# A kernel of eight layers on one core: the output product moves to the bank of queries and keys, copies change places, and the two mixtures fill their gate chains with products

## The chip, the cores and the metric

The kernel runs on one core of a Trainium2 chip. The metric is the device time of one execution in microseconds (us). Before the change three timed runs took 1647.21, 1647.35 and 1652.68 us, median 1647.35. The profiled execution, from which all rows below are taken, took 1640.3 us; its span, from the first to the last instruction, is 1638.5 us, so 1.8 us lie around the span. Engines are named as in the profile: PE (TensorE matmul), PEld (TensorE weight load), DVE (VectorE), ACT (ScalarE), POOL (GpSimd).

## The reference

The input is 8 sequences of 256 tokens of 128 numbers, 2048 tokens in all, and a context of the same shape. Four attention layers and four feed-forward layers follow each other, each with a layer norm in front and a residual sum behind:

```
x = x + L0_xattn(layernorm(x), ctx, ctx)              # 16 heads of 8, causal
x = x + L0_ffn(layernorm(x), W1, b1, W2, b2)          # ternary weights, gelu
x = x + L1_xattn(layernorm(x), ctx, mask, ...)        # 16 heads of 64, row mask
x = x + L1_ffn(layernorm(x), ...)                     # product keys, top 8
x = x + L2_xattn(ctx, layernorm(x), ...)              # 16 heads of 8, biases, causal
x = x + L2_ffn(layernorm(x), w_red, wg, W1, b1, W2, b2)   # mixture, 1 of 8 experts, gelu
x = x + L3_xattn(layernorm(x), ctx, ctx, mask, ...)   # 16 heads of 64, key mask
x = x + L3_ffn(layernorm(x), gate_w, we_*, ws_*)      # mixture, 2 of 8 experts, 2 shared, silu
```

The two attention layers with 16 heads of 64 (L1 and L3) are the wide layers. In outline, for one head: `softmax(q @ k.T * 64**-0.5 + mask) @ v`, then all heads times the output weights. The mixture of L2 takes for each token the expert of the largest gate: `o = (gelu(x @ W1[e] + b1[e]) @ W2[e] + b2[e]) * score`. The mixture of L3 takes the two largest of 8 gates, each expert with a capacity of 640 tokens in order of arrival, and adds two shared experts that every token passes: `sh = silu(x @ ws_gate.T) * (x @ ws_up.T) @ ws_down.T`. Everything is float32.

## The kernel before, in words

All engines run a program written out by hand, in order, with semaphores between them: an instruction behind a wait stands still with its engine. The layers are stages one after the other: raw, ffn0, rows (the wide layer L1, 207 to 545 us), ffn1, bias, ffn2 (the mixture L2, 1011 to 1160), keys (the wide layer L3, 1161 to 1490), ffn3 (the mixture L3, 1493 to the end).

**A wide layer** goes over 8 batches (one sequence of 256 tokens each), 8 pairs of heads in a batch, two pairs in a step, so 4 steps u = 0 to 3 in a batch. Batch 0 and batch 7 are written out, batches 1 to 6 are a loop. A step of PE (`step` in `wide_tensor`) is: the scores of two pairs (L932, into banks 0 to 3), the product of weights and values of the step before last (`weighted`, L969, bank 6), one product of queries and keys (L898 and L899, bank 7), the transposes of a pair of the step before (L947: its four for i = 0 into bank 4, its four for i = 1 into bank 5), a product for the values (L911, bank 6), a second one of queries and keys, and a second pair's transposes. Step 2 then turns the normalised x of the next batch (`norm`, L888), and step 1 does the output product of the batch before (`out_product`, L919, 16 matmuls into bank 5). Because bank 5 is also the bank of the transposes for i = 1, the output product waits until ACT has copied these out (`w_pt[1]`, ACT L1046), and in the next step the transposes wait until DVE has added the product to x (`w_added`, DVE L1121).

DVE in a step: the maxima of both pairs (L1137, 8 instructions), the inverse of the first pair's sums (L1143), the copy of queries and keys (L1107), in step 0 the statistics of the next batch (L1257 to L218), the inverse of the second pair's sums, the copy of the first transposes (`copy_pt`, L1150, bank 4), the copy of the values (L1114), in step 2 the next batch's normalisation (`normalise`, L1096), the second `copy_pt`, in step 2 the copy of the turned x (`norm_out`, L1103) and the context, in step 1 the addition of the output product. ACT does the exponentials (L1036), the other half of the transposes (L1046), every second copy of queries and keys (L1027) and the heads' results (L1053). POOL multiplies by the inverses (L1213, two instructions of 128x512 for a pair) and does the Newton rounds for the norm's root (L1298 to L1304, four small instructions a round): two rounds in step 0, the third in step 1.

**A mixture** first normalises all 16 tiles, turns them (L1490), and makes the gate logits (L1898). Then DVE runs a chain of small instructions (the gate chain): the largest gates, their indices, a hand-over to ACT for the exponential (L1928), the sums and weights, and a split in three bf16 parts (L1992 to L1996). PE turns these (L1920) and ACT copies them to `gT` (L1931), which every group of 512 tokens needs to spread its gates (L2068, L2139). While DVE is in the chain, PE does four products ahead in ffn2 and two units' in ffn3, then waits. Four groups follow, group 0 written out, the others a loop. In ffn2 a group has 16 halves of experts: an up product (L1880), ACT's gelu, DVE's product with the gate, a down product (L2060). In ffn3 a group has 10 units, 8 experts and 2 shared ones: two up products (L1888 and L1889), ACT's silu (L2162), DVE's product with the up result (L2182) and with the gate (L2186), a down product (L2130); a shared unit has only one DVE product (L2189).

## Time and profile before

| | |
|---|---|
| timed runs, median of 3 | 1647.35 us (1647.21 to 1652.68) |
| profiled execution | 1640.3 us, span 1638.5 us, mean granted clock 0.958 |
| PE busy | 1413.3 us, 86% of the span |
| DVE, ACT, POOL busy | 1022.6, 898.7, 690.4 us |
| the chain that ended last | PE 61%, DVE 17%, ACT 12%, issue 8%, POOL 2% |
| one batch in the loop of the keys stage | 39.91 us |
| one group in the loop of ffn3 | 29.09 us |

Busy time is the time in which an engine had an instruction in work. A matmul of float32 is recorded as two PE records (x2 for one matmul), and matmuls overlap in the pipeline: eight records that last 1.04 us together are followed by the next instruction after less than that. In brackets stands the idle time of the engine ahead of an instruction and who ended it.

### The profile page before, as it was taken

Reading aid. Unit: us, or ns where it says so; the run is one execution under the profiler, and the core shown is the slowest. Engines: PE = TensorE matmul, PEld = TensorE weight load, DVE = VectorE, ACT = ScalarE, POOL = GpSimd, SP = SyncE. Lnnn points to the kernel's source line nnn. Section 1 sums busy time; section 2 is a strip of 40 time slices with the busy share of each in tenths; the row PEclk is TensorE's granted clock in tenths of the full one; section 3 lists DMA queues with packets and bytes.
Section 4 is the critical chain, followed back from the end, with each engine's and each line's share of the span. In section 5 each row is a group of like instructions: output and inputs, shape, how many; then the busy total and the mean of one; then the engine's idle time right before and its main releaser. Section 6 shows DMA issues by size and latency. Waiting matters only on the chain.

```text
span 1638.5 us, 30033 instructions
## 1 busy us (share of the span) xinstructions
PE 1413.3 (86%) x9437; PEld 937.4 (57%) x9449; DVE 1022.6 (62%) x3380; ACT 898.7 (55%) x1867; POOL 690.4 (42%) x1056
## 2 busy tenths in 40 slices
PE   5996889999998577868778895899899999996998
PEld 2443457777766476767654443444576777664343
DVE  5653366666665799998955554433566666655444
ACT  3665456666665477777746663333566666661222
POOL 5341144444443589989853331000344444441000
PEclk9999899999999689998999997999999999997999
DMA  2016000000000000000000000000000000000000
GB/s 66 17 49 252 4 4 5 3 3 3 3 3 1 26 1 1 1 0 0 1 1 1 1 2 1 26 1 0 4 4 4 3 3 6 0 1 1 7 6 13
DMA packets 12665, 21.76 MB, mean 13 GB/s; under 512 B 3088, under 2 KB 9120, under 8 KB 11936
## 3 DMA queue, kind: packets, MB, share of 16 engines
q1 hardware_dynamic: 12576, 20.63, 3.5%
q8 instruction: 49, 0.80, 0.2%
q14 instruction: 40, 0.33, 0.1%
HBM read 19.58 MB, written 1.05 MB: 13 GB/s over the span
## 4 chain that ended last, share of the span: by engine, by line
PE 61%; DVE 17%; ACT 12%; issue 8%; POOL 2%; DVEq 0%; ACTq 0%; DMA 0%; SPq 0%; POOLq 0%
PE bank L932 7%; PE bank L969 6%; PE bank L947 5%; DVE sb_both L1841 4%; PE bank L919 4%; ACT sb_both L1036 4%; PE bank L1880 3%; PE bank L2060 3%; PE bank L898 3%; PE bank L409 2%; PE bank L1888 2%; PE bank L451 2%; PE bank L1889 2%; PE bank L899 2%; PE bank L2130 2%
## 5 line engine op out<-in xcount | busy, mean ns | idle before, releaser
L1213 POOL TENSOR_TENSOR sb_both<-sb_both,sb_winv 128x512 f32<-128x512 f32 x256 | 260.8, 1040 | 323.7 <-DVE sb_winv L1143 323.7
L1036 ACT ACTIVATE sb_both<-sb_both,sb_wneg 128x256 f32<-128x256 f32 x512 | 253.0, 495 | 151.0 <-DVE sb_wneg L1137 150.9
L1768 POOL TENSOR_TENSOR sb_KM<-sb_OT 128x1024 f32<-128x1024 f32 x128 | 240.2, 1913 | 31.8 <-DVE sb_both L1841 27.8
L1672 PE MATMUL bank<-sb_ident,sb_both 128*128 128x128 f32 x1024 | 139.4, 286 | 59.3 <-DVE sb_both L1841 37.0
L1137 DVE CUSTOM_DVE_ANT_0 sb_both<-bank,sb_pen 128x256 f32<-128x256 f32 x512 | 182.1, 420 | 0.0
L1298 POOL TENSOR_TENSOR sb_ntmp<-sb_rstd 128x2 f32<-128x2 f32 (+2 forms) x123 | 24.2, 197 | 340.6 <-DVE sb_rstd L218 335.3
L1841 DVE SCALAR_TENSOR_TENSOR sb_both<-sb_KM,sb_best,bank 128x1024 f32<-128x1024 f32 x128 | 158.4, 1273 | 11.3 <-ACT bank L1743 11.3
L1672 PEld LDWEIGHTS bank<-sb_ident,sb_both 128*128 128x128 f32 x1024 | 119.2, 147 | 73.6 <-DVE sb_both L1841 47.4
L1743 ACT ACTIVATE bank<-sb_KM 128x1024 f32<-128x1024 f32 x128 | 129.6, 1023 | 35.3 <-DVE sb_both L1841 30.2
L947 PE MATMUL bank<-sb_ident,sb_both 128*128 128x128 f32 x1024 | 134.4, 274 | 12.2 <-DVE sb_QT L1150 12.1
L947 PEld LDWEIGHTS bank<-sb_ident,sb_both 128*128 128x128 f32 x1024 | 116.3, 141 | 36.0 <-issue 20.0
L969 PE MATMUL bank<-sb_QT,sb_VP 128*64 128x256 f32 x1024 | 127.7, 392 | 3.2 <-DVE sb_QT L1150 3.2
L932 PE MATMUL bank<-sb_KM 64*128 64x256 f32 x1024 | 128.1, 390 | 0.0
L932 PEld LDWEIGHTS bank<-sb_KM 64*128 64x128 f32 x1024 | 93.8, 187 | 19.6 <-issue 8.6
L1150 DVE COPY sb_QT<-bank 128x512 f32<-128x512 f32 x128 | 88.1, 688 | 24.3 <-PE bank L947 24.0
L969 PEld LDWEIGHTS bank<-sb_QT,sb_VP 128*64 128x64 f32 x1024 | 69.8, 139 | 52.1 <-issue 20.8
L1036 ACT ACTIVATION_READ_ACCUMULATOR sb_both<-sb_both,sb_wneg 128x1 f32 x512 | 95.9, 187 | 0.0
L1046 ACT ACTIVATE sb_QT<-bank 128x512 f32<-128x512 f32 x128 | 75.1, 587 | 35.3 <-PE bank L947 35.3
L2116 DVE TENSOR_TENSOR sb_both<-bank,sb_both 128x512 f32<-128x512 f32 x64 | 44.0, 691 | 74.1 <-ACT sb_both L2095 48.7
L692 DVE TENSOR_REDUCE sb_VP<-bank 128x4 f32<-128x1024 f32 (+1 forms) x48 | 58.7, 1223 | 36.2 <-PE bank L415 36.0
L583 ACT ACTIVATE sb_xnT_all<-bank 128x1024 f32<-128x1024 f32 x48 | 49.0, 1022 | 52.2 <-PE bank L415 52.2
L2095 ACT ACTIVATE sb_both<-bank,sb_f1b 128x512 f32<-128x512 f32 x64 | 43.6, 687 | 61.5 <-PE bank L1880 61.5
(273 smaller groups left out, 2731.0 us busy)
## 6 DMA issues: line engine op xcount, KB each, us to landing
sb_ctxT_in<-in_ctxT SPq DMA_DIRECT2D x24, 128.0 KB, 2.3
sb_F<-in_F SPq DMA_DIRECT2D x2, 1024.0 KB
sb_XO<-in_ctx SPq DMA_DIRECT2D x8, 128.0 KB, 2.0
sb_WKQ<-in_WKQ SPq DMA_DIRECT2D x1, 1024.0 KB, 9.0
sb_W1ALL<-in_ctxT SPq DMA_DIRECT2D x1, 1024.0 KB, 4.7
sb_xn_all<-in_keymask SPq DMA_DIRECT2D x1, 1024.0 KB, 4.3
out_x<-sb_x SPq DMA_DIRECT2D x4, 256.0 KB, 2.3
sb_x<-in_x SPq DMA_DIRECT2D x1, 896.0 KB, 4.7
```

The source lines that it names most:

```text
L932: last = pe.matmul(s[:, h, i, :], QK[rows, t, 0, i * P:(i + 1) * P], QK[rows, t, 1, :], start=True, stop=True)
L947: last = pe.transpose(bank[4 + i][:, n * P:(n + 1) * P], PRW[:, t % 4, h, i, kt * P:(kt + 1) * P], ident[:])
L969: last = pe.matmul(bank[6][rows, (t % 2) * SEQ:(t % 2 + 1) * SEQ], VW[:, kt, (2 * t + h) * 64:(2 * t + h + 1) * 64], PTW[:, t % 2, h, kt, ...
L1036: last = act.activation(p, p, ACT.Exp, scale=-1.0, bias=wneg[:, t % 4, h, i:i + 1], accum_out=wsum[:, t % 4, h, i:i + 1])
L1046: act.activation(PTW[:, t % 2, :, :, P:2 * P], bank[5][:].rearrange("p (h i q) -> p h i q", h=2, i=TPB), ACT.Copy).then_inc(w_pt[1], 1)
L1137: dve.tensor_tensor_reduce(PRW[:, t % 4, h, i, :], s[:, h, i, :], mask, -1.0, BIG, ALU.add, ALU.min, wneg[:, t % 4, h, i:i + 1]).then_inc( ...
L1150: dve.tensor_copy(PTW[:, t % 2, :, :, 0:P], bank[4][:].rearrange("p (h i q) -> p h i q", h=2, i=TPB))\
L1213: pool.tensor_tensor(p, p, winv[:, t % 4, :, i:i + 1].broadcast_to([P, 2, SEQ]), ALU.mult).then_inc(w_norm, 1)
L1672: last = pe.matmul(weight_bank(c), gated[:, h % 4, c * P:(c + 1) * P], ident[:], is_transpose=True, start=(h == 0 and c % 4 == 0), stop=(h ...
L1743: act.activation(sig_bank(h), pairsum[:, h % 4, :], ACT.Sigmoid).then_inc(sig_ready, 1)
L1768: pool.tensor_tensor(dst, s[:, h, 0, :].unsqueeze(2).broadcast_to([P, NK, NK]), s[:, h, 1, :].unsqueeze(1).broadcast_to([P, NK, NK]), ALU. ...
L1841: dve.scalar_tensor_tensor(out=gated[:, h % 4, :], in0=pairsum[:, h % 4, :], scalar=best[:, t % 2, h, TOPK - 1:TOPK], in1=sig_bank(h), op0 ...
```

## The change

In the wide layers the output product goes to bank 7, the bank of queries and keys, and waits for the copy of the sixth pair's queries and keys in place of ACT's copy of the transposes; the next product that uses bank 7 after it, that of pair 6 in step 2, waits for the addition. On DVE the first `copy_pt` stands ahead of the second inverse, and `normalise` moves from the middle of step 2 to step 1, ahead of the addition. POOL does all three Newton rounds in step 0.

In ffn2, PE does all 16 up products of group 0 while the gate chain runs, ACT puts their gelu into 16 buffers of their own (`first_acts`, in KM and VP), and takes the gate's exponential after the fifth gelu and the copies of `gT` after the eleventh. In ffn3 the two shared experts leave the groups and are done for all tokens ahead of them, among the steps of the gate chain: PE's up products, ACT's silu and a copy of the up result, POOL's product, PE's down product (with the tokens on the rows, so nothing has to be turned back), ACT's copy, and POOL's addition to x. A group has then 8 units.

```diff
@@ wide_tensor
+                if j == 6 and not known_below(b, 1):
+                    pe.wait_ge(w_added, A.batches + b)
                 pe.matmul(bank[7][:, 0:SEQ], WQ[:, j * P:(j + 1) * P], xnT[:], start=True, stop=True)
...
-            def out_product(b, turned):
+            def out_product(b, copied):
                 pe.wait_ge(w_ot, heads(b + 1, 0))
-                pe.wait_ge(w_pt[1], A.pairs + turned)
+                pe.wait_ge(w_qk_out, A.pairs + copied)
...
-                        last = pe.matmul(bank[5][:, i * D:(i + 1) * D], OT[:, j, i * P:(i + 1) * P], WO[:, j, :],
+                        last = pe.matmul(bank[7][:, i * D:(i + 1) * D], OT[:, j, i * P:(i + 1) * P], WO[:, j, :],
...
-                    if t == 2 and i == 1 and not known_below(b, 1):
-                        pe.wait_ge(w_added, A.batches + b)
...
-                    out_product(b - 1, PAIRS * b + 2)
+                    out_product(b - 1, PAIRS * b + 6)
@@ wide_vector, step
+                if behind or u >= 1:
+                    bt, ut = steps_back(b, u, 1)
+                    copy_pt(bt, 2 * ut)
                 inverses(b, 2 * u + 1)
                 if u == 3 and more:
                     penalty(b + 1)
-                if behind or u >= 1:
-                    bt, ut = steps_back(b, u, 1)
-                    copy_pt(bt, 2 * ut)
                 if u < 3:
                     values(b, u + 1)
                 elif more:
                     values(b + 1, 0)
-                if u == 2 and more:
-                    normalise(b + 1)
                 if behind or u >= 1:
                     copy_pt(bt, 2 * ut + 1)
+                if u == 1 and more:
+                    normalise(b + 1)
@@ wide_pool, step
                 if u == 0 and part != "last":
-                    rsqrt(pool, 0, TPB, A.ln + b + 1, [0, 1])
-                if u == 1 and part != "last":
-                    rsqrt(pool, 0, TPB, A.ln + b + 1, [2])
+                    rsqrt(pool, 0, TPB, A.ln + b + 1)
@@ ffn2 and ffn3
+    EXP_AFTER2, GATE_AFTER2 = 4, 10
+    def shared_down(pe, g):
+        pe.wait_ge(sh_prod, 2 * g + 2)
+        if g >= 2:
+            pe.wait_ge(sh_out, g - 1)
+        for i in range(TPG):
+            for u in range(2):
+                last = pe.matmul(bank[4 + g % 2][:, i * P:(i + 1) * P],
+                                 gated_ring[:, (2 * g + u) % 4, i * P:(i + 1) * P], SD[:, u, :],
+                                 start=(u == 0), stop=(u == 1))
+        last.then_inc(sh_down, 1)
+    def shared_act(act, q):
+        u = q % 2
+        act.wait_ge(sh_up, q + 1)
+        if q >= 4:
+            act.wait_ge(sh_prod, q - 3)
+        act.activation(act_ring[:, q % 4, :], bank[2 * u][:], ACT.Silu)
+        act.activation(shared_u[:, q % 4, :], bank[2 * u + 1][:], ACT.Copy).then_inc(sh_act, 1)
...
+        for q in range(2 * GROUPS):
+            product(q)                      # POOL: shared_u * act_ring -> gated_ring
+            if q >= 5 and q % 2 == 1:
+                add((q - 5) // 2)           # POOL: x += shared_out
...
@@ tensor2
-        gate_tensor(pe, A)
+        gate_logits(pe, A)
+        for n in range(16):
+            up2(pe, 0, n)
+            if n == GATE_AFTER2:
+                gate_turn(pe, A, 4)
+        pe.wait_ge(gT_ready, 2)
@@ scalar2, body
+                if known_zero(g) and n == EXP_AFTER2:
+                    gate_exp(act, A)
+                if known_zero(g) and n == GATE_AFTER2:
+                    gate_out(act, A, 4)
@@ scalar3
-        gate_scalar(act, A)
+        shared_act(act, 0)
+        shared_act(act, 1)
+        gate_exp(act, A)
+        shared_act(act, 2)
...
+        shared_evac(act, 1)
+        gate_out(act, A, 6)
+        shared_act(act, 6)
...
```

The first place is DVE in step 2 and step 1 of a batch of the keys stage (`sb_QT` is where the transposed weights go, `sb_VP` the values, `sb_xn` the normalised x of the next batch, `sb_xnT` its transpose). Step 2 before:

```order
L1107 COPY sb_KM<-bank 128x512
L1143 RECIPROCAL sb_winv<-sb_wsum 128x4
L1149 REGISTER_ALU
L1150 COPY sb_QT<-bank 128x4x128
L1111 REGISTER_ALU
L1114 COPY sb_VP<-bank 128x512
L1094 ISA
L1096 TENSOR_SCALAR sb_xn<-sb_x,sb_mv,sb_rstd 128x128 x2
L1149 ISA
L1150 COPY sb_QT<-bank 128x4x128
L1100 REGISTER_ALU
```

Step 1 of the changed kernel, on DVE, from the same copy of queries and keys to the addition:

```order
L1107 COPY sb_KM<-bank 128x512
L1149 REGISTER_ALU
L1150 COPY sb_QT<-bank 128x4x128
L1143 RECIPROCAL sb_winv<-sb_wsum 128x4
L1111 REGISTER_ALU
L1113 REGISTER_ALU
L1114 COPY sb_VP<-bank 128x512
L1149 ISA
L1150 COPY sb_QT<-bank 128x4x128
L1094 ISA
L1096 TENSOR_SCALAR sb_xn<-sb_x,sb_mv,sb_rstd 128x128 x2
L1117 REGISTER_ALU
```

The first copy to `sb_QT` moved ahead of the inverse, and the two instructions that write `sb_xn` stood between the values and the second copy in step 2; they now stand behind the second copy of step 1, with the wait of the addition (L1117) next.

The second place is ACT in ffn2 between the four copies of the turned x and group 0's end. In the changed kernel (`sb_g_e` is the exponential of the gates; ACT_TABLE_LOAD changes the function table; the kernel before has one in this stage, ahead of the first gelu and behind the copies of `gT`):

```order
L1499 ACTIVATE sb_xnT_all<-bank 128x512 x4
L2155 ACT_TABLE_LOAD
L2155 ACTIVATE sb_KM<-bank,sb_f1b 128x512 x5
L1978 ACT_TABLE_LOAD
L1978 ACTIVATE sb_g_e<-sb_g_t 128x128
L2155 ACT_TABLE_LOAD
L2155 ACTIVATE sb_KM<-bank,sb_f1b 128x512 x3
L2155 ACTIVATE sb_VP<-bank,sb_f1b 128x512 x3
L1984 ACTIVATE sb_gT<-bank 128x1024 x2
L2155 ACTIVATE sb_VP<-bank,sb_f1b 128x512 x5
L2163 ACTIVATE sb_outT<-bank 128x512
```

The gate's exponential moved behind five gelus, and it has a table change on each side. In ffn3 it stands in the same way behind two silus and two copies.

## Rows read from the trace of the kernel before

**Rows 1.** Windows: span, then PE, PEld, DVE, ACT, POOL busy, clock, DMA.
```profile
1256.77:1296.68 39.91, 38.04 (x266) 28.02 (x267) 26.63 (x111) 24.79 (x80) 18.57 (x28) 1.00 0.01 3
...
1507.00:1511.00 4.00, 4.00 (x18) 1.99 (x16) 3.51 (x15) 0.00 (x0) 0.00 (x0) 0.50 0.00 0
...
1518.00:1524.60 6.60, 5.87 (x8) 2.47 (x9) 1.97 (x3) 0.00 (x0) 0.00 (x0) 0.50 0.00 0
...
1545.27:1574.36 29.09, 28.34 (x70) 12.49 (x72) 13.05 (x19) 6.57 (x11) 0.00 (x0) 1.00 0.02 9
```
**Rows 2.** Timeline of PE, keys stage: start, duration, instruction, [idle before <-releaser].
```profile
1269.61 0.43 PE L888 MATMUL bank<-sb_ident,sb_xn 128*128 128x128 f32 x2 [0.69 <-DVE sb_xn L1096]
...
1274.74 1.04 PE L947 MATMUL bank<-sb_ident,sb_both 128*128 128x128 f32 x8
1275.62 1.02 PE L911 MATMUL bank<-sb_WV,sb_ctxT 128*128 128x512 f32 x2
...
1286.39 1.06 PE L947 MATMUL bank<-sb_ident,sb_both 128*128 128x128 f32 x8 [0.40 <-DVE sb_QT L1150]
...
1296.68 3.81 PE L919 MATMUL bank<-sb_WO,sb_OT 128*128 128x128 f32 x32 [0.78 <-ACT sb_QT L1046]
```
**Rows 3.** Timeline of DVE in the same batch.
```profile
1268.14 1.33 DVE L1096 TENSOR_SCALAR sb_xn<-sb_x,sb_mv,sb_rstd 128x128 f32 x2
...
1285.39 0.17 DVE L1143 RECIPROCAL sb_winv<-sb_wsum 128x4 f32<-128x4 f32 x1
1285.56 0.69 DVE L1150 COPY sb_QT<-bank 128x512 f32<-128x512 f32 x1
...
1300.66 0.43 DVE L1121 TENSOR_TENSOR sb_x<-bank,sb_x 128x256 f32 x1 [4.46 <-PE bank L919]
```
**Rows 4.** Timeline of POOL in the same batch.
```profile
1285.64 2.04 POOL L1213 TENSOR_TENSOR sb_both<-sb_both,sb_winv 128x512 f32<-128x512 f32 x2 [0.68 <-DVE sb_winv L1143]
1287.64 0.19 POOL L1298 TENSOR_TENSOR sb_ntmp<-sb_rstd 128x2 f32<-128x2 f32 x1
...
1289.55 0.19 POOL L1304 TENSOR_TENSOR sb_rstd<-sb_rstd,sb_ntmp 128x2 f32<-128x2 f32 x1
```
**Rows 5.** Timeline of ACT in the same batch.
```profile
1294.97 0.60 ACT L1027 ACTIVATE sb_KM<-bank 128x512 f32<-128x512 f32 x1 [0.62 <-PE bank L899]
```
**Rows 6.** Timeline of PE at the gate chain and group 0's start of ffn2.
```profile
1028.73 5.85 PE L1880 MATMUL bank<-sb_xnT_all,sb_F 128*128 128x512 f32 x8
1035.89 1.07 PE L1920 MATMUL bank<-sb_identB,sb_QT 128*128 128x128 bf16 x16 [1.31 <-DVE sb_QT L1996]
1038.77 0.38 PE L2068 MATMUL bank<-sb_gT,sb_sel 128*128 128x512 bf16 x1 [1.81 <-ACT sb_gT L1931]
...
1041.26 1.13 PE L2060 MATMUL bank<-sb_both,sb_F 128*128 128x512 f32 x2 [1.47 <-DVE sb_both L2116]
```
**Rows 7.** Timeline of ACT, the table change ahead of the first gelu of ffn2.
```profile
1038.50 1.28 ACT L2095 ACT_TABLE_LOAD   x1
1039.80 2.42 ACT L2095 ACTIVATE sb_both<-bank,sb_f1b 128x512 f32<-128x512 f32 x4
```
**Rows 8.** Timeline of DVE, the first instruction behind the exponential in ffn2.
```profile
1033.49 0.29 DVE L1969 TENSOR_REDUCE sb_gs_z<-sb_g_e 128x16 f32<-128x128 f32 x1
```
**Rows 9.** Timeline of PE in ffn3: gate chain, first down product, last of group 0.
```profile
1506.53 0.29 PE L1906 MATMUL bank<-sb_picks,sb_before 128*128 128x128 bf16 x1 [5.29 <-DVE sb_picks L1967]
...
1515.60 0.38 PE L2139 MATMUL bank<-sb_gT,sb_sel 128*128 128x512 bf16 x1 [1.81 <-ACT sb_gT L1931]
1518.73 2.07 PE L2130 MATMUL bank<-sb_both,sb_WD 128*128 128x512 f32 x2 [2.75 <-DVE sb_both L2186]
...
1545.27 1.13 PE L2130 MATMUL bank<-sb_both,sb_SD 128*128 128x512 f32 x2 [0.61 <-DVEq L2192]
...
1560.07 0.38 PE L2139 MATMUL bank<-sb_gT,sb_sel 128*128 x1
...
1562.86 0.38 PE L2139 MATMUL bank<-sb_gT,sb_sel 128*128 x1
```

More of the change, by code:

```diff
@@ L1883, in up3 @@
     def up3(pe, g, n):
-        if not (known_zero(g) and n < 2):
-            pe.wait_ge(prod_step, UNITS * g + n - 1)
-        wgate, wup, _ = unit_weights(n)
-        pe.matmul(bank[2 * (n % 2)][:], wgate, xnT_all[:, bass.ts(g, GROUP)], start=True, stop=True)
-        pe.matmul(bank[2 * (n % 2) + 1][:], wup, xnT_all[:, bass.ts(g, GROUP)],
-                  start=True, stop=True).then_inc(up_done[3], 1)
-    def gate_tensor(pe, A):
+        if known_zero(g) and n < 2:
+            pe.wait_ge(sh_act, 2 * GROUPS - 1 + n)
+        else:
+            pe.wait_ge(prod_step, EXPERTS * g + n - 1)
@@ new lines, in up3, with shared_up @@
+        pe.matmul(bank[2 * (n % 2)][:], WG[:, n, :], xnT_all[:, bass.ts(g, GROUP)], start=True, stop=True)
+        pe.matmul(bank[2 * (n % 2) + 1][:], WU[:, n, :], xnT_all[:, bass.ts(g, GROUP)],
+                  start=True, stop=True).then_inc(up_done[3], 1)
+    def shared_up(pe, q):
+        g, u = q // 2, q % 2
+        if q >= 2:
+            pe.wait_ge(sh_act, q - 1)
+        pe.matmul(bank[2 * u][:], SG[:, u, :], xnT_all[:, g * GROUP:(g + 1) * GROUP], start=True, stop=True)
+        pe.matmul(bank[2 * u + 1][:], SU[:, u, :], xnT_all[:, g * GROUP:(g + 1) * GROUP],
+                  start=True, stop=True).then_inc(sh_up, 1)
@@ new lines, in shared_evac, with pool3, product, add @@
+    def shared_evac(act, g):
+        act.wait_ge(sh_down, g + 1)
+        act.activation(shared_out[:, g, :], bank[4 + g % 2][:], ACT.Copy).then_inc(sh_out, 1)
+    def pool3(pool, A):
+        def product(q):
+            pool.wait_ge(sh_act, q + 1)
+            if q >= 4:
+                pool.wait_ge(sh_down, (q - 4) // 2 + 1)
+            pool.tensor_tensor(gated_ring[:, q % 4, :], shared_u[:, q % 4, :], act_ring[:, q % 4, :], ALU.mult)\
+                .then_inc(sh_prod, 1)
+        def add(g):
+            pool.wait_ge(sh_out, g + 1)
+            xg = x[:, TPG * g:TPG * g + TPG, :]
+            pool.tensor_tensor(xg, xg, shared_out[:, g, :].rearrange("p (i d) -> p i d", i=TPG), ALU.add)\
+                .then_inc(sh_added, 1)
+        for q in range(2 * GROUPS):
+            product(q)
+            if q >= 5 and q % 2 == 1:
+                add((q - 5) // 2)
+        add(GROUPS - 2)
+        add(GROUPS - 1)
@@ L1900, in gate_tensor, with gate_counts, gate_turn @@
         last.then_inc(lg_done, 1)
-        if k == 1:
-            pe.wait_ge(count_done, 1)
-            flat = picks[:].rearrange("p t e -> p (t e)")
-            width = TILES * EXPERTS
-            pe.matmul(bank[7][:, 0:width], before[:], flat, start=True, stop=True)
-            for n in range(1, TILES):
-                last = pe.matmul(bank[7][:, n * EXPERTS:width], onesB[:], flat[:, 0:width - n * EXPERTS],
-                                 start=False, stop=True, skip_group_check=True)
-            last.then_inc(count_done, 1)
-        if k == 0:
-            for n in range(UPS_AHEAD2):
-                up2(pe, 0, n)
-        else:
-            for n in range(UNITS_AHEAD3):
-                up3(pe, 0, n)
-        pe.wait_ge(parts_ready, k + 1)
+    def gate_counts(pe):
+        pe.wait_ge(count_done, 1)
+        flat = picks[:].rearrange("p t e -> p (t e)")
+        width = TILES * EXPERTS
+        pe.matmul(bank[7][:, 0:width], before[:], flat, start=True, stop=True)
+        for n in range(1, TILES):
+            last = pe.matmul(bank[7][:, n * EXPERTS:width], onesB[:], flat[:, 0:width - n * EXPERTS],
+                             start=False, stop=True, skip_group_check=True)
+        last.then_inc(count_done, 1)
+    def gate_turn(pe, A, first):
+        pe.wait_ge(parts_ready, A.index - 1)
         for i in range(TILES):
-            home = bank[4 + i // 8][:].bitcast(BF16)
+            home = bank[first + i // 8][:].bitcast(BF16)
             last = pe.transpose(home[:, (i % 8) * P:(i % 8 + 1) * P], parts[:, i, :], identB[:])
@@ L2125, in tensor3 @@
         norm_tensor(pe, A)
[L2126 removed]
+        gate_logits(pe, A)
+        for q in range(4):
+            shared_up(pe, q)
+        gate_counts(pe)
+        shared_down(pe, 0)
+        shared_up(pe, 4)
+        shared_up(pe, 5)
+        shared_down(pe, 1)
+        gate_turn(pe, A, 6)
+        shared_up(pe, 6)
+        shared_up(pe, 7)
+        shared_down(pe, 2)
+        shared_down(pe, 3)
+        pe.wait_ge(gT_ready, 4)
+        pe.wait_ge(sh_out, GROUPS - 1)
         def down(g, n):
[L2129 to L2130 removed]
+            pe.wait_ge(gated_done[1], EXPERTS * g + n + 1)
+            pe.matmul(bank[6][:], WD[:, n, :], gated_ring[:, n % 4, :], start=(n == 0), stop=(n == EXPERTS - 1))\
               .then_inc(down_done[1], 1)
         def body(g):
[L2134 to L2142 removed]
+            for n in range(EXPERTS):
+                if known_zero(g) and n == 1:
+                    pe.wait_ge(sh_out, GROUPS)
+                if not (known_zero(g) and n < 2):
+                    pe.wait_ge(gated_done[1], EXPERTS * g + n - 1)
+                pe.matmul(bank[4 + n % 2][:], sel[:, n, :], gT[:, bass.ts(g, GROUP)],
+                          start=True, stop=True).then_inc(bc_done[1], 1)
+                up3(pe, g, n)
                 if n == 1 and not known_zero(g):
@@ L2146, in body @@
                     down(g, n - 1)
-            down(g, UNITS - 1)
+            down(g, EXPERTS - 1)
         groups(pe, body)
@@ L2226, in pool @@
             pool1(pool_, A)
+        if A.kind == "ffn3":
+            pool3(pool_, A)
     F.early_stats = early_stats
```

101 lines of the change are left out of this document (50 added, 51 removed).

## The prediction

> **What bounds the kernel now.** I read the windows first, then the timeline of PE with its idle times, then the other engines around each idle time. In the loop of a wide layer a batch takes 39.91 us, and PE has an instruction in work for 38.04 of them at the full clock [rows 1]; DVE, ACT and POOL are at 26.6, 24.8 and 18.6 us. So PE is the bound, and the 1.87 us left are three idle times that the timeline names: 0.69 us ahead of the turning of the next batch's x, 0.40 us ahead of a second transpose, 0.78 us ahead of the output product [rows 2]. They add up to 1.87 exactly, so nothing else of size is lost there. In the mixtures PE stands still around the gate chain: 1.31, 1.81 and 1.47 us in ffn2 [rows 6], and 5.29, 1.81 and 2.75 us in ffn3 [rows 9]. In ffn3 each group also ends in 0.61 us of waiting.
>
> **Wide layers, the output product.** It waits for ACT's copy of bank 5 [rows 2], which can only start when the transposes are through. In bank 7 it waits for the sixth copy of queries and keys, which ACT begins at 1294.97 and ends at 1295.57 [rows 5]. PE would be free at about 1295.65: the idle time goes but for a few hundredths. With it goes the tail of the pipeline: eight transposes last 1.04 us, but 0.88 us later the next instruction starts [rows 2], so a stop behind them costs 0.16 us more than the idle time shown. 0.78 + 0.16 = 0.94 us. The next user of bank 7 is the first product of step 2, behind scores and weighting, 3.9 us later; the addition takes 0.43 us right behind the product [rows 3]. That new wait is covered by over 3 us.
>
> **The norm.** The two instructions of 1.33 us stand ahead of the second copy in step 2, and PE waits for them, 0.69 us [rows 2, 3]. In step 1 they come in front of the addition, where DVE is idle for 4.46 us [rows 3]; they cost nothing there. They need the Newton rounds to be through. The second pair's multiplication on POOL starts up to 0.6 us later, since its inverse now stands behind a copy (0.69 us): 1285.64 becomes about 1286.25, it ends at 1288.3, and three rounds at 1.1 us (two last from 1287.64 to 1289.74) end at 1291.6 [rows 4]. The norm asks at about 1296: 4 us to spare. POOL's next pair waits in any case for the first inverse of step 1, some eight maxima into that step, and its product is turned only a step later. Gain 0.69 + 0.16 = 0.85 us.
>
> **The copy ahead of the inverse.** In step 0 the copy starts 0.17 us earlier, at the inverse's place, 1285.39 [rows 3], and PE's idle 0.40 us shrinks by that. In steps 1 to 3 the inverse waits for ACT's exponentials in any case, so the copy fits in front of it. Small gaps ahead of the second transposes there, and the slower refilling of the pipeline behind each stop, bear no name in the trace; I put 0.3 us on them, an estimate from the other stops' tails of 0.16 us.
>
> Sum for a batch: 0.94 + 0.85 + 0.17 + 0.3 = 2.3 us (2.26), lower bound 1.6 (idle times alone), upper 2.5. The loop has six batches; batch 0 has the norm but no output product and batch 7 the reverse, so I count 7.2 batches in each of two wide layers: 14.4 x 2.3 = 33 us (23 to 36).
>
> **ffn2.** Nothing is added on PE, only moved. Twelve up products of 0.86 us (half a pair of up and down products, of which the sixteen pieces below 1041.26 are full) go from group 0 into the gaps. What ACT does now sets the pace. The fifth gelu ends at about 1036.1; a change of tables takes 1.28 us [rows 7] and the exponential 0.3, so it ends at 1037.7 where it was through at 1033.4 before. From there DVE needs 1035.89 - 1033.49 = 2.4 us to the parts [rows 6, 8]: 1040.2. The next table change ends at 1039.0, and the tenth up product, which needs the sixth gelu's bank, starts at 1039.75 instead of 1038.7: one idle time of 1.05 us. PE turns the parts at 1041.5, when they have long been ready. ACT copies gT behind the eleventh gelu until 1044.6, which PE needs at 1046.7. The first down product comes at about 1047.9. Before it came at 1041.26, with twelve up products of 0.86 us = 10.3 us still to do, that is 1051.6 in this count. Gain 3.7 us (0.8 to 4.6).
>
> The price of a change of tables decides this term. The row shows 1.28 us, with the gelu 1.30 us behind the start of the load [rows 7]. The Trainium skill, "ScalarE: Activation LUTs", section "What ACT_TABLE_LOAD costs", gives about 1.28 us for the load plus some 1.38 us to drain, 2.66 us for every switch; by that the two added changes of ffn2 would delay the tenth up product by 2.8 us and the gain would be 0.9 us, and in ffn3 about 2 us would go. The trace shows no such drain ahead of or behind the load, so I go by the row.
>
> **ffn3.** A unit takes 1562.86 - 1560.07 = 2.79 us on PE, of which 0.22 is the spreading of the gate; a shared unit has 2.57 [rows 9]. Two leave each group: 5.14 us of 29.09 [rows 1]. But the group now ends with an expert, whose last down product waits for two products of DVE in a row in place of one: 0.61 becomes about 1.4 us, +0.8. A group gets 4.35 us shorter, four groups 17.4 us. Ahead of them come 16 up products, 13.8 us, and 32 small down products at 3.75 / 16 = 0.234 us as the output product has them [rows 2], 7.5 us: together 21.3 us. They fill 5.29 + 1.81 + 2.75 = 9.85 us of idle time. Because PE stood still, the first down product of group 0 took 2.07 us where 1.13 is the rule [rows 9]: the granted clock was 0.50, its lower level of 1.2 GHz, from 1507 to 1511 and from 1518 to 1524.6 us, with 4.00 + 5.87 us of PE in work [rows 1], of which half is the price: 5 us. In the changed kernel only the first two shared pairs run so, about 2.5 us. Rests remain: 0.7 us ahead of the last shared down product (its last product is POOL's, 1.02 us [rows 4], behind ACT), 0.4 us at the first expert, 0.3 elsewhere. The exponential is 3 us late and the parts come at 1514.5, PE asks at 1517.8. Sum: -17.4 - 9.85 - 5 + 21.3 + 2.5 + 1.4 = -7 us (-11 to 0).
>
> POOL's eight products lie beside DVE's chain. The Trainium skill, "SBUF — State Buffer", section "SBUF: two separate sides", says that POOL and a VectorE instruction with two SBUF inputs lock each other out of a shared pair of ports for whole instructions. No row here shows it; if it held, the chain could wait for up to three products, 3 us, which the 3.3 us to spare just cover.
>
> **Sum.** 33 + 3.7 + 7 = 43.7 us off the profiled execution's 1640.3 us, that is 1596.6 us. The timed runs' median lies 7 us above the profiled execution, so the forecast for the median is 1647.35 - 43.7 = 1603.6, rounded to 1603 us, 2.7% faster.
>
> **Rivals.**
> *A wait takes the place of the ones removed* (the copy of queries and keys by ACT for the output product, or DVE's addition, or the heads' copy ahead of the values): half the wide gain, 16 us, goes, and the time is 1619. For it: ACT's copy ends within 0.1 us of the point where PE asks. Against: all other slacks that I find are 0.2 us and more in a step of 8.4 us.
> *The mixtures give nothing*, because of the clock, the tables or the longer end of a group: 1647.35 - 33 = 1614. For it: the term of ffn3 is a difference of large numbers.
> *The moves in the wide layers don't do what they say*, PE's idle times only get other names: 1647.35 - 11 = 1636.
> *Slower.* The norm in step 1 waits for POOL's three rounds, and behind it on DVE stand the addition and the maxima of step 2; PE's product of pair 6 waits for the addition. If POOL's twelve small instructions came 4 us late, DVE would hold the loop, and from 7.5 us late on each of 14 batches would lose 3.1 us more than the mixtures and the rest give: 1650 to 1680, say 1660. Against: 4 us to spare before the first 0.1 us is lost, and POOL is busy for 18.6 of 39.9 us [rows 1].
>
> **How the numbers follow.** Forecast 0.72, half the wide gain 0.11, mixtures give nothing 0.09, moves without effect 0.04, slower 0.04. The range of 8 in 10 takes the bounds of the wide term (23 to 36) and of the mixtures (1 to 15), and some us by which executions of one kernel differ here: 1590 to 1619. A measurement of this kernel can tell about 0.5%, 8 us, from no change. Only the slower rival and a part of the fourth case lie at or above 1639: faster 0.93, same 0.03, slower 0.04.
>
> **What would show it.** A batch of the loop should last 37.6 us, with only 0.2 to 0.3 us of idle time left on PE, ahead of a second transpose in step 0; the output product with no idle time ahead of it, or one named by the copy of queries and keys. DVE's norm should come about 0.1 us behind a copy, with POOL's last round well before. In ffn2 one idle time of about 1 us within the up products and the first down product 18 to 20 us behind the first up product. In ffn3 three groups of 24.7 us with 1.4 us of waiting at the end, and the first expert's down product about 37 us behind the first turning of x. I am wrong if the loop's period stays above 38.5 us, or if a table change costs clearly over 1.3 us.

## The result and the profile after

The changed kernel takes 1603.43 us, median of four runs (1600.34 to 1607.1), beside 1647.28 us for the kernel before, also of four (1646.96 to 1652.68): the ratio is 0.9723, with a 95% interval of 0.970 to 0.9746. That is 43.85 us less. The profiled execution took 1600.34 us with a span of 1598.5 us, 40.0 us less than the one of before.

The windows of the changed kernel, columns as in [rows 1]: a batch in the loop of the keys stage, the gate logits of ffn2, the first shared up products of ffn3, and a group in the loop of ffn3.

```profile
1236.51:1274.32 37.81, 37.41 (x268) 28.20 (x267) 26.22 (x112) 24.78 (x80) 18.60 (x29) 1.00 0.01 3
1010.43:1017.11 6.68, 6.68 (x33) 6.68 (x33) 0.11 (x1) 1.88 (x2) 0.00 (x0) 0.50 0.42 158
1468.09:1473.90 5.81, 5.81 (x8) 2.50 (x9) 5.38 (x54) 1.08 (x2) 0.78 (x1) 0.51 0.00 1
1519.02:1543.54 24.52, 23.13 (x59) 10.24 (x61) 11.66 (x17) 5.37 (x9) 0.00 (x0) 1.00 0.03 11
```

A batch lost 2.10 us [rows 1], a group 4.57. The timeline of PE in a batch of the loop, at the places of [rows 2]:

```profile
1265.08 1.06 PE L947 MATMUL bank<-sb_ident,sb_both 128*128 128x128 f32 x8 [0.40 <-DVE sb_QT L1150]
...
1285.44 1.04 PE L947 MATMUL bank<-sb_ident,sb_both 128*128 128x128 f32 x8
1286.31 0.38 PE L888 MATMUL bank<-sb_ident,sb_xn 128*128 128x128 f32 x2
...
1311.27 1.04 PE L947 MATMUL bank<-sb_ident,sb_both 128*128 128x128 f32 x8
1312.14 3.82 PE L921 MATMUL bank<-sb_WO,sb_OT 128*128 128x128 f32 x32
```

The turning of the next x (L888) and the output product (L921) follow their transposes by 0.87 us with no idle time; the 0.40 us of step 0 stands as it stood. Summed from the starts of such rows in both traces, the 2.10 us are 0.97 for the output product, 0.92 for the norm, 0.13 and 0.08 for two gaps without a name ahead of second transposes.

By stage, from the first turning of x to the next stage's first (us; rows and keys are the wide layers):

| | rows | ffn1, bias | ffn2 | keys | ffn3 | before rows |
|---|---|---|---|---|---|---|
| before | 335.0 | 477.9 | 141.5 | 332.2 | 144.9 | 206.9 |
| changed | 318.4 | 477.9 | 139.7 | 315.1 | 138.0 | 209.5 |
| saved | 16.6 | 0.0 | 1.8 | 17.2 | 7.0 | -2.6 |

The last column is a warning for all that follows: no edit touches the work ahead of rows, yet in the thirteen profiled executions of this study it ended anywhere from 206.9 to 215.1 us. So whole times of single executions differ by up to 8 us without any edit; lengths of stages and periods of loops are what tells kernels apart. The loop periods repeat to 0.02 us.

### The profile page after: what moved, and what is told of

It reads as the page before. It is cut to its first block, busy times and chain, and to the rows that moved or that the text cites. A ratio compares the mean times of both kernels' runs of the same rounds, so it can differ in the third digit from the quotient of the medians.

```text
span 1598.5 us, 30106 instructions
## 1 busy us (share of the span) xinstructions
PE 1406.6 (88%) x9483; PEld 945.5 (59%) x9497; DVE 1023.4 (64%) x3372; ACT 909.5 (57%) x1883; POOL 706.3 (44%) x1068
## 3 DMA queue, kind: packets, MB, share of 16 engines
HBM read 19.58 MB, written 1.05 MB: 13 GB/s over the span
## 4 chain that ended last, share of the span: by engine, by line
PE 68%; DVE 15%; ACT 9%; issue 6%; POOL 1%; DVEq 0%; DMA 0%; ACTq 0%; SPq 0%; POOLq 0%
PE bank L934 7%; PE bank L969 7%; PE bank L947 6%; DVE sb_both L1846 4%; PE bank L900 4%; PE bank L921 4%; PE bank L1879 3%; PE bank L2118 3%; PE bank L901 3%; PE bank L913 3%; PE bank L409 2%; PE bank L451 2%; ACT sb_KM L598 2%; ACT sb_both L598 2%; ACT bank L1748 2%
## 5 line engine op out<-in xcount | busy, mean ns | idle before, releaser
L969 PE MATMUL bank<-sb_QT,sb_VP 128*64 128x256 f32 x1024 | 124.6, 385 | 3.2 <-DVE sb_QT L1150 1.6
L969 PEld LDWEIGHTS bank<-sb_QT,sb_VP 128*64 128x64 f32 x1024 | 68.6, 136 | 50.9 <-issue 21.9
L1027 ACT ACTIVATE sb_KM<-bank 128x512 f32<-128x512 f32 x64 | 38.2, 597 | 58.2 <-PE bank L901 58.1
L1107 DVE COPY sb_KM<-bank 128x512 f32<-128x512 f32 x64 | 44.1, 690 | 39.8 <-PE bank L901 39.8
```

The lines of the kernel that those rows point to most:

```text
L969: last = pe.matmul(bank[6][rows, (t % 2) * SEQ:(t % 2 + 1) * SEQ], VW[:, kt, (2 * t + h) * 64:(2 * t + h + 1) * 64], PTW[:, t % 2, h, kt, ...
```

## The experiments

Two parts of the change alone, each timed several times beside the kernel before, which took 1649.31 us there.

**wide_only.** The file before with every edit of the wide layers and none of the mixtures.

> The kernel before with the wide layers' part alone. My theory: the edits of the wide layers and of the mixtures don't touch each other, so rows and keys are as short as in the changed kernel (318.4 and 315.1 us instead of 335.0 and 332.2), ffn2 and ffn3 stay at 141.5 and 144.9 us; 34 us off, 1613. Rival, that a part of the mixtures' gain comes from the other state in which the clock reaches them: ffn2 or ffn3 moves by 2 us or more without any edit of its own.

Measured: 1615.42 us, ratio 0.979 (0.9756 to 0.9823), 33.9 us off. rows 318.3, keys 316.4 us, and a batch of keys 37.82. But ffn2, in which nothing is changed, took 143.97 us where it had taken 141.53. The rival's condition holds. The timeline of its PE shows where:

```profile
1014.87 1.12 PE L1488 MATMUL bank<-sb_ident,sb_xn_all 128*128 128x128 f32 x4 [0.66 <-DVE sb_xn_all L1481]
1015.78 6.83 PE L1896 MATMUL bank<-sb_gateW,sb_xnT_all 128*128 128x8 f32 x32
1022.46 6.73 PE L1878 MATMUL bank<-sb_xnT_all,sb_F 128*128 128x512 f32 x8
```

and the same place in the trace of the kernel before:

```profile
1023.57 0.66 PE L1490 MATMUL bank<-sb_ident,sb_xn_all 128*128 128x128 f32 x4 [0.66 <-DVE sb_xn_all L1483]
1024.07 4.81 PE L1898 MATMUL bank<-sb_gateW,sb_xnT_all 128*128 128x8 f32 x32
```

The gate logits took 6.83 us at a granted clock of 0.50 (1.2 GHz) and 4.81 us at 0.75, that is partly at 2.4 GHz, behind the same 8.51 and 0.66 us of idle time. In twelve of thirteen profiled executions they took 6.8 us; the one of before was the exception. What lies ahead of them is the same, so it is the moment at which the clock comes back that differs.

**mix_only.** The file before with the edits of ffn2 and ffn3 alone.

> The kernel before with the mixtures' part alone. My theory: ffn2 and ffn3 take 139.7 and 138.0 us as in the changed kernel, all else stays; 9 us off, 1638. Of ffn2, 2 us hang on whether its gate logits run at the lower clock for 4.8 or 6.8 us, which no edit decides: 137.7 if they take 4.8 us here. Rival: the mixtures give nothing by themselves, 1647.

Measured: 1637.96 us, ratio 0.9933 (0.9907 to 0.9959), 11.35 us off. The stages: ffn2 140.0 us with the logits at 6.8, ffn3 136.5 us (1.5 us less than expected, see the clock below); a batch of keys 39.92. The two parts add up to within 1.4 us: 33.9 + 11.35 = 45.2 beside 43.85.

The next six undo, move or leave out one thing in the changed kernel, one execution each; they are read by the lengths of stages and loop periods.

**bank5.**
```diff
-                pe.wait_ge(w_qk_out, A.pairs + copied)
+                pe.wait_ge(w_pt[1], A.pairs + copied)
...
-                        last = pe.matmul(bank[7][:, i * D:(i + 1) * D], OT[:, j, i * P:(i + 1) * P], WO[:, j, :],
+                        last = pe.matmul(bank[5][:, i * D:(i + 1) * D], OT[:, j, i * P:(i + 1) * P], WO[:, j, :],
...
+                    if t == 2 and i == 1 and not known_below(b, 1):
+                        pe.wait_ge(w_added, A.batches + b)
...
```


> The changed kernel with the output product back in bank 5, with its old waits, on all engines. My theory: PE waits again 0.78 us for ACT's copy of the transposes, and with the pipeline's tail a batch of the loop takes 0.97 us more, 38.8 instead of 37.81. Rival, that the other edits of the wide layers already give the copy its time: the idle time is under 0.4 us and the batch under 38.3 us.

Measured: a batch of 38.76 us, +0.94, with this row of its PE:

```profile
1287.94 3.81 PE L919 MATMUL bank<-sb_WO,sb_OT 128*128 128x128 f32 x32 [0.78 <-ACT sb_QT L1046]
```

The idle time of [rows 2] is back to the hundredth: the bank was its cause, and the other edits don't lend it time.

**norm2.**
```diff
+                if u == 2 and more:
+                    normalise(b + 1)
                 if behind or u >= 1:
                     copy_pt(bt, 2 * ut + 1)
-                if u == 1 and more:
-                    normalise(b + 1)
```


> The changed kernel with the normalisation back in step 2, ahead of the second copy; POOL still does all three rounds in step 0. My theory: its two instructions lie again beside POOL's products of 1.02 us and take 1.33 us instead of 0.59, since the two engines shut each other out; PE waits 0.7 us for them, and a batch takes 0.92 us more, 38.7. Rival, that the third round on POOL in step 1 was what slowed them: they take 0.59 us, PE waits under 0.1 us, and a batch takes 37.9.

Measured: a batch of 38.48 us, +0.66; the rows of its DVE, PE and POOL:

```profile
1295.11 1.40 DVE L1096 TENSOR_SCALAR sb_xn<-sb_x,sb_mv,sb_rstd 128x128 f32 x2
```
```profile
1296.64 0.43 PE L888 MATMUL bank<-sb_ident,sb_xn 128*128 128x128 f32 x2 [0.44 <-DVE sb_xn L1096]
```
```profile
1294.39 2.04 POOL L1213 TENSOR_TENSOR sb_both<-sb_both,sb_winv 128x512 f32<-128x512 f32 x2 [0.22 <-DVE sb_winv L1143]
```

The two instructions take 1.40 us beside POOL's products and end 0.08 us behind them, with all Newton rounds in step 0: the rival is out. The idle time is 0.44 and not 0.7 us, since DVE comes to the norm 0.3 us earlier, counted from PE's transposes: before, the first of the two instructions was held until POOL's second product ended (1.08 us) and the second followed it (0.33 us); here the first slips in (0.40 us) and only the second is held (1.08 us). All the durations of that line in the keys stage, in the trace before and in the one after (ns, min/median/max), show the same:

```profile
L1096 DVE TENSOR_SCALAR sb_xn<-sb_x,sb_mv,sb_rstd x14: 333/704/1091, 1188.4 to 1428.8; 128x128 f32 x12, 128x128 f32<-128x128 f32 x2
```
```profile
L1096 DVE TENSOR_SCALAR sb_xn<-sb_x,sb_mv,sb_rstd x12: 338/341/346, 1199.1 to 1388.4; 128x128 f32 x12
```

**copy_behind.**
```diff
-                if behind or u >= 1:
-                    bt, ut = steps_back(b, u, 1)
-                    copy_pt(bt, 2 * ut)
                 inverses(b, 2 * u + 1)
...
+                if behind or u >= 1:
+                    bt, ut = steps_back(b, u, 1)
+                    copy_pt(bt, 2 * ut)
```


> The changed kernel with the first copy of transposes behind the second inverse again, as before. The prediction's account: 0.17 us of step 0 and most of 0.3 us of unnamed gaps come back, a batch of 38.2 to 38.3 us. What the changed kernel's trace says: the idle time of 0.40 us in step 0 did not move, so only the gaps of 0.13 and 0.08 us ahead of second transposes can come back, 38.0 at most. Rival: the order of these two makes no difference at all, 37.81.

Measured: a batch of 37.99 us in keys (+0.18) and 37.97 in rows (+0.08), with the same 0.40 us in step 0. So in the loop the order gives the small gaps and nothing in step 0. Its DVE there, and below it that of the changed kernel:

```profile
1315.56 0.17 DVE L218 TENSOR_SCALAR sb_rstd<-sb_vbits 128x2 int32<-128x2 uint32 x1
1315.64 0.17 DVE L1143 RECIPROCAL sb_winv<-sb_wsum 128x4 f32<-128x4 f32 x1
1315.80 0.69 DVE L1150 COPY sb_QT<-bank 128x512 f32<-128x512 f32 x1
```
```profile
1264.00 0.17 DVE L218 TENSOR_SCALAR sb_rstd<-sb_vbits 128x2 int32<-128x2 uint32 x1
1264.24 0.69 DVE L1150 COPY sb_QT<-bank 128x512 f32<-128x512 f32 x1
```

The copy starts 0.24 us behind L218 with or without the inverse between them. The inverse lay in a gap that is there anyway.

Outside the loop the order is worth more. The keys stage took 321.0 us beside 315.1, the rows stage 322.5 beside 318.4, and most of that lies in the last batch, where PE has no products for a next step to do meanwhile: from the seventh output product to the eighth it is 31.88 us in keys and 32.30 in rows, beside 28.40 and 28.39. PE and DVE of copy_behind there, in keys:

```profile
1458.66 1.59 PE L947 MATMUL bank<-sb_ident,sb_both 128*128 128x128 f32 x8 [2.35 <-DVE sb_QT L1150]
1461.05 3.68 PE L969 MATMUL bank<-sb_QT,sb_VP 128*64 128x256 f32 x16 [0.79 <-DVE sb_QT L1150]
```
```profile
1457.75 0.18 DVE L1143 RECIPROCAL sb_winv<-sb_wsum 128x4 f32<-128x4 f32 x1 [2.08 <-ACT sb_both L1036]
```

and PE and DVE of the changed kernel:

```profile
1442.56 0.63 PE L947 MATMUL bank<-sb_ident,sb_both 128*128 128x128 f32 x4 [0.51 <-POOL sb_both L1213]
1444.07 0.63 PE L947 MATMUL bank<-sb_ident,sb_both 128*128 128x128 f32 x4 [0.89 <-ACT sb_QT L1046]
1445.49 1.95 PE L969 MATMUL bank<-sb_QT,sb_VP 128*64 128x256 f32 x16 [0.79 <-issue]
```
```profile
1441.72 0.69 DVE L1150 COPY sb_QT<-bank 128x512 f32<-128x512 f32 x1 [0.32 <-PE bank L947]
```

In the old order the copy stands behind an inverse that waits 2.08 us for ACT's exponentials, and PE stands still for 2.35 us; in the new order the stop is 0.51 and 0.89 us. The product behind it (L969) ran at a granted clock of 0.50 in copy_behind and at 1.00 in the changed kernel, 3.68 us instead of 1.95. Over all thirteen profiled executions, both wide stages, it took 3.3 to 3.7 us in six of six stages with the old order (before, mix_only, copy_behind) and in two of twenty with the new one (rows of norm2, 3.48; keys of stats_late, 3.60). So the longer stop and the lower clock behind it go with the order of these two instructions.

**stats_late.**
```diff
-                if u == 0 and more:
-                    norm_stats(dve, A, b + 1)
                 if behind or u >= 1:
                     bt, ut = steps_back(b, u, 1)
                     copy_pt(bt, 2 * ut)
                 inverses(b, 2 * u + 1)
+                if u == 0 and more:
+                    norm_stats(dve, A, b + 1)
```


> The changed kernel with the statistics of the next batch, in step 0, behind the first copy and the second inverse instead of ahead of them. My theory: the copy of bank 4 waits for DVE's 1.5 us of statistics, so the idle time of 0.40 us ahead of the second transposes goes, with 0.16 us of tail: a batch of 37.25 us, and some 8 us off the whole. Rival, that the delay only moves: the copy of the values and the second copy come 1.5 us later, the maxima of step 1 start late, and a batch takes 37.8 us or more.

Measured: a batch of 37.63 us, 0.19 less instead of 0.56. The 0.40 us is gone, and a new wait stands in step 1. DVE, then PE:

```profile
1316.33 0.36 DVE L212 TENSOR_SCALAR sb_veps<-sb_mv 128x2 f32<-128x2 f32 x1
1316.61 0.16 DVE L213 TENSOR_SCALAR sb_vhalf<-sb_mv 128x2 f32<-128x2 f32 x1
1316.80 0.90 DVE L215 TENSOR_SCALAR sb_vbits<-sb_veps 128x2 uint32<-128x2 uint32 x1
...
1318.54 0.68 DVE L1150 COPY sb_QT<-bank 128x512 f32<-128x512 f32 x1
```
```profile
1319.55 1.95 PE L969 MATMUL bank<-sb_QT,sb_VP 128*64 128x256 f32 x16 [0.30 <-DVE sb_QT L1150]
```

Instructions of 0.17 us took 0.36 and 0.90 us beside POOL's products (1315.63 to 1317.67), so the second copy came late. The wait moved, as the rival had it, but the trace puts 0.9 us of DVE's delay down to POOL; stats_early, below, tests that. Not all small instructions were held: the norm's statistics (L1255) took 0.29 and 0.28 us and their merging (L1259) 0.18 and 0.15 us beside the first of these products, as they do without one.

**parts_first.**
```diff
         for q in range(2 * GROUPS):
+            if q == 2:
+                pool.wait_ge(parts_ready, A.index - 1)
             product(q)
@@ tensor3 (scalar3 in the same order)
-        shared_down(pe, 1)
         gate_turn(pe, A, 6)
         shared_up(pe, 6)
         shared_up(pe, 7)
+        shared_down(pe, 1)
```


> The changed kernel, ffn3: POOL's products from the third on wait for the parts of the gates, and PE turns the parts ahead of the second shared down product. My theory, that POOL's products hold up DVE's chain by shutting it out of SBUF: from the first instruction behind the exponential to the end of the parts 5.2 us, as in the kernel before, instead of 9.2; no DVE instruction of the chain over 0.3 us; PE's 0.97 us ahead of the turning goes, and ffn3 is 1 to 2 us shorter. Rival, that the long instructions have another cause (weight loads, ACT's reads): the chain still takes 8 us or more.

In the changed kernel the chain behind the exponential looks like this on DVE:

```profile
1477.39 0.28 DVE L2022 TENSOR_REDUCE sb_gs_z<-sb_g_e 128x16 f32<-128x128 f32 x1 [2.87 <-ACT sb_g_e L1978]
...
1479.88 1.37 DVE L2035 TENSOR_TENSOR sb_g_oh<-sb_g_oh,sb_gs_w 128x128 f32<-128x128 f32 x1
1481.29 1.24 DVE L2036 TENSOR_TENSOR sb_g_comb<-sb_g_oh 128x128 f32<-128x128 f32 x1
...
1483.48 1.34 DVE L2046 TENSOR_TENSOR sb_g_r<-sb_g_comb,sb_QT 128x128 f32<-128x128 f32 x1
...
1485.44 1.17 DVE L2049 CAST sb_QT<-sb_g_r 128x128 bf16<-128x128 f32 x1
```

and POOL at the same time:

```profile
1479.84 2.55 POOL L1930 TENSOR_TENSOR sb_both<-sb_VP,sb_both 128x512 f32<-128x512 f32 x2 [2.75 <-ACT sb_VP L1919]
1483.40 1.27 POOL L1930 TENSOR_TENSOR sb_both<-sb_VP,sb_both 128x512 f32<-128x512 f32 x1 [1.02 <-ACT sb_VP L1919]
1485.12 1.41 POOL L1930 TENSOR_TENSOR sb_both<-sb_VP,sb_both 128x512 f32<-128x512 f32 x1 [0.45 <-ACT sb_VP L1919]
```

Each long instruction of DVE starts 0.05 to 0.32 us after a product of POOL has started and ends 0.08 to 0.15 us behind it; their neighbours take 0.29 us or less. With the products held back, DVE of parts_first:

```profile
1475.44 0.28 DVE L2024 TENSOR_REDUCE sb_gs_z<-sb_g_e 128x16 f32<-128x128 f32 x1 [1.49 <-ACT sb_g_e L1980]
...
1477.93 0.29 DVE L2037 TENSOR_TENSOR sb_g_oh<-sb_g_oh,sb_gs_w 128x128 f32<-128x128 f32 x1
...
1480.41 0.23 DVE L2051 CAST sb_QT<-sb_g_r 128x128 bf16<-128x128 f32 x1
```

The chain takes 1480.64 - 1475.44 = 5.20 us instead of 1486.61 - 1477.39 = 9.22. The expectation holds for the chain, and the rival is out. PE turns the parts without waiting. From the first turning of x to the first expert's down product it is 36.86 us; bank5 and group_end, whose ffn3 front is the changed kernel's and whose clock came back at the same point, take 37.82: 0.96 us gained, the 0.97 us of idle time, at the lower end of the 1 to 2 us expected.

**no_switch.**
```diff
-        act.activation(gt["e8"][:], gt["t1"][:], ACT.Exp).then_inc(gexp_done, 1)
+        act.activation(gt["e8"][:], gt["t1"][:], ACT.Gelu if A.index == 2 else ACT.Exp).then_inc(gexp_done, 1)
```


> The changed kernel, with the exponential of ffn2's gate replaced by a gelu, so the gates have other values; it leaves out two table changes of ACT in ffn2. By the row of 1.28 us for a change: ACT's sixth gelu comes 2.6 us earlier, PE's idle time of 0.96 us ahead of the tenth up product goes, and ffn2's group 0 ends 1.1 us earlier. If a change cost 2.66 us (load and drain), the sixth gelu would come 5.3 us earlier, and more than 2 us of idle time of PE would have to be found in the changed kernel that goes here.

ACT of the changed kernel around the exponential of ffn2:

```profile
1023.05 0.69 ACT L2155 ACTIVATE sb_KM<-bank,sb_f1b 128x512 f32<-128x512 f32 x1 [0.17 <-PE bank L1879]
1023.75 1.28 ACT L1978 ACT_TABLE_LOAD   x1
1025.05 0.31 ACT L1978 ACTIVATE sb_g_e<-sb_g_t 128x128 f32<-128x128 f32 x1
1025.37 1.28 ACT L2155 ACT_TABLE_LOAD   x1
1026.67 1.84 ACT L2155 ACTIVATE sb_KM<-bank,sb_f1b 128x512 f32<-128x512 f32 x3
```

and of no_switch:

```profile
1029.99 0.69 ACT L2155 ACTIVATE sb_KM<-bank,sb_f1b 128x512 f32<-128x512 f32 x1 [0.17 <-PE bank L1879]
1030.58 0.30 ACT L1978 ACTIVATE sb_g_e<-sb_g_t 128x128 f32<-128x128 f32 x1
1030.85 0.69 ACT L2155 ACTIVATE sb_KM<-bank,sb_f1b 128x512 f32<-128x512 f32 x1
```

Measured: from the fifth gelu to the sixth 3.62 us become 0.86: two changes cost 2.76 us, 1.38 each. PE's 0.96 us ahead of the tenth up product is gone; ffn2's stage is 139.1 us beside 139.7, a smaller gain than 1.1, since the low clock lasted longer into the up products: eleven of them took 11.5 us, where at 0.86 us each they take 9.5; in the changed kernel the first nine took 9.2 where they would take 7.7.

Then two that should better the kernel, and all three good ones together.

**group_end.**
```diff
                 up3(pe, g, n)
+                if n == 0 and not known_zero(g):
+                    down(g - 1, EXPERTS - 1)
...
-            down(g, EXPERTS - 1)
         groups(pe, body)
+        down(GROUPS - 1, EXPERTS - 1)
...
```


> The changed kernel, ffn3: a group's last down product stands behind the next group's first pair of up products on PE, and ACT copies the group's result behind the next group's first silu. My theory: the 1.28 us that PE waits at the end of groups 0 to 2, with 0.16 us of tail, is filled by 1.94 us of work; a group of the loop takes 24.51 - 1.44 = 23.1 us, 4.3 us off in all; the last group still ends with its wait. Rival, that the wait moves: the copy of the result comes later, the silu behind it too, and the group's second or third down product waits instead, 24.0 us or more.

The part that is left out moves ACT's copy of the group's result behind the next group's first silu.

Measured: a group of 22.77 us, 1.75 less, 0.3 more than expected, and ffn3 131.2 us beside 136.4 in bank5, whose front ran at the same clock; PE has no named idle time in the loop's groups. The rival is out.

**stats_early.**
```diff
                 maxima(b, 2 * u + 1)
+                if u == 2 and more:
+                    normalise(b + 1)
                 inverses(b, 2 * u)
...
-                if u == 0 and more:
-                    norm_stats(dve, A, b + 1)
...
                 if u == 1 and more:
-                    normalise(b + 1)
+                    norm_stats(dve, A, b + 1)
@@ wide_pool
-                if u == 0 and part != "last":
+                if u == 1 and part != "last":
```


> The changed kernel with the next batch's statistics in step 1, in DVE's idle time ahead of the addition of the output product, POOL's rounds in step 1, and the normalisation in step 2 between the maxima and the first inverse, where POOL is idle. My theory: the copy in step 0 has nothing ahead of it and PE's 0.40 us go with 0.16 us of tail, and none of DVE's small instructions lies beside a product of POOL: a batch of 37.25 us. Rival, that the first inverse of step 2, 0.6 us later, makes POOL's products and so a transposition late: PE waits in step 3, 37.6 us or more.

Measured: a batch of 37.23 us, no idle time on PE in it. DVE's small instructions are back at 0.17 us, the norm at 0.60:

```profile
1312.45 0.17 DVE L215 TENSOR_SCALAR sb_vbits<-sb_veps 128x2 uint32<-128x2 uint32 x1
...
1318.84 0.60 DVE L1096 TENSOR_SCALAR sb_xn<-sb_x,sb_mv,sb_rstd 128x128 f32 x2
```

The same work as in stats_late, but where POOL is idle, gives the full 0.58 us. The rival is out.

**best.** parts_first, group_end and stats_early together, timed six times.

> The changed kernel with three edits together: the parts ahead of POOL's third product, the group's last down product behind the next group's first up products, and the statistics in step 1. If each holds alone and they don't meet: 1 to 2 us, 4.3 us and 14 times 0.56 = 7.8 us off the changed kernel's 1603.4, that is 1589 to 1590. If the statistics' place gives only the 0.19 us a batch that the place behind the inverse gave: 1595. Rival, that the three give nothing together: 1603.

Measured: 1589.48 us (1584.71 to 1593.04) beside 1648.58 us, ratio 0.9626 (0.960 to 0.9653). It beats both kernels; its interval does not touch the changed kernel's. Batches of 37.23 and groups of 22.77 us: the three edits don't meet.

## Why the prediction was right, point by point

The forecast was 1603 us (its sum gives 1603.65) and the median is 1603.43; the savings were put at 43.7 us and are 43.85. Which waits would go, and where PE would stand instead, came out as described, but that the total fits to half a microsecond is luck: single executions of the changed kernel lie between 1600.3 and 1607.1 us, and wrong terms below cancel. The terms came out so:

- **Output product, 0.94 us a batch**: 0.97 in the trace, 0.94 by bank5. Right, the 0.16 us for the pipeline's tail too; the new wait for the addition costs nothing.
- **The norm, 0.85**: 0.92 in the trace. The size was right, the reading behind it incomplete. The 1.33 us of [rows 3] were taken for the norm's own length; alone it takes 0.59. The rest was POOL's product.
- **The copy ahead of the inverse, 0.17**: failed in step 0. PE's 0.40 us did not move. copy_behind shows why: the copy starts 0.24 us behind L218 in either order. The start of an instruction, less that of the one ahead, is not the price of the one ahead. What the prediction did not count is the last batch, where the same order saves 3.5 and 3.9 us a layer by copy_behind, and 2.4 and 2.7 between the two kernels' profiled executions.
- **Unnamed gaps, 0.3**: 0.21 in the trace, 0.18 in keys and 0.08 in rows by copy_behind.
- **The count of batches, 7.2 a layer**: mis-sized. The terms left 2.1 us a batch in keys and 2.0 in rows instead of 2.3, yet keys saved 17.2 us, which is 8.2 times 2.1. The stretch up to the first output product saved 2.3 us and the tail behind the seventh 2.4. Of that tail 1.6 us are one product (L969) that ran at half the clock before, 3.59 us instead of 1.95, and 0.8 us the shorter stops ahead of it. The product ran slow in every stage with the old order of copy and inverse and in two of twenty with the new one, so most of the 1.6 us belongs to the edit too, though the new order does not rule the slow clock out. Two errors cancelled: 33 us forecast, 33.8 measured.
- **ffn2, 3.7**: 1.8 us between the two profiled executions, but with unlike clocks under the logits. Against wide_only, whose logits took the same 6.8 us, it is 143.97 - 139.72 = 4.25 us, and 2.6 to 4.3 over the kernels with this ffn2 and both table changes. One idle time of 0.96 us ahead of the tenth up product (1.05 forecast), the first down product 18.6 us behind the first up product (18 to 20).
- **The table change**: the row's 1.28 us, or 1.38 by the difference that no_switch makes. The Trainium skill, "ScalarE: Activation LUTs", section "What ACT_TABLE_LOAD costs", adds a drain of about 1.38 us to the load. No run here shows it: two changes and their rests cost 2.76 us, where it would make them 5.3.
- **ffn3, 7**: 7.0 between the two profiled executions, and luck in part: over the eight executions with this ffn3 the stage took 136.4 to 141.0 us, beside 144.9 and 145.3 for the two with the old one, so the saving is 4 to 9 us, depending on when the clock comes back. The group's 24.7 us is 24.52, its wait at the end 1.28 (1.4); the rest ahead of the last shared down product 0.74 (0.7), at the first expert 0.21 (0.4); the shared up products lost about 2.9 us to the clock (2.5). The first down product came 39.3 us behind the first turning, not 37.
- **The 3.3 us to spare for the parts**: failed. DVE's chain was 4.0 us longer and PE waited 0.97 us. The prediction said of the lock between POOL and DVE that no row showed it. That was wrong: the norm's 1.33 us in [rows 3] was such a row. In the trace of the kernel before, the first of its two instructions took 1.08 us and ended 0.08 us behind this pair of POOL's, which ends at 1269.14:

```profile
1267.10 2.04 POOL L1213 TENSOR_TENSOR sb_both<-sb_both,sb_winv 128x512 f32<-128x512 f32 x2 [0.22 <-DVE sb_winv L1143]
```

  POOL's product was taken at 1.02 us, the price with a broadcast operand [rows 4]; with two full operands it takes 1.26.

The lock is what the Trainium skill says in "SBUF — State Buffer", section "SBUF: two separate sides": whichever of a GpSimd instruction and a VectorE one with two SBUF inputs, or in a mode that uses both ports, starts first keeps the shared pair for the whole instruction. The traces agree, also for DVE instructions with one tensor input: the cast (L2049, 1.17 us instead of 0.23), the norm (L1096), and L215 with two elements in a row (0.90 instead of 0.17). Not held up are copies from a PSUM bank (0.69 us everywhere) and, among those that work on SBUF alone, the norm's statistics (0.28 us), their merging (0.15) and the inverse of 128x4 (0.18).

What stays open is what makes the clock come back at one moment or another: with one and the same ffn3 front, the first down product came 37.8 to 42.4 us behind the first turning of x in nine profiled executions, and no edit orders them. For the tail of a wide layer the order of copy and inverse goes with it, but what in the longer stop does it is not shown. No run here was made for that.

## What to carry to other kernels

Where an instruction takes longer than its twin elsewhere, look at what the other engines do in that microsecond before its length is taken for its price; DVE's scalings, casts and two-operand instructions on SBUF belong where POOL is idle. A stop of PE costs its idle time and some 0.16 us of tail, and it goes when the thing waited for gets another buffer, or the waiting instruction stands behind other work. Compare stages and loop periods, not the whole of two executions, and only where the clock was the same.
